# Batches of edges on every second step of the first group's chain, and turned rows of the early mixes loaded by pairs of tiles

## The reference

```
xn = layernorm(x)
msg = (xn @ weight[rel])[rel_type, src] * norm * sigmoid(gate[rel_type, src])
agg = segment_sum(msg, dst)                     # one row of 256 per edge, added by node
mix = linear attention over all nodes: k and v normalised per head, q @ (k'v / n) @ w_out + b_out
x2 = x + relu(agg) + mix
out = x2 + moe(layernorm(x2))                   # 8 experts, gelu, the best 2 of 8 by a softmax
```

## Time and profile before

| what | value |
| --- | --- |
| median of the runs, before | 1965.0 us (3 runs, 1964.9 to 1967.81) |
| profiled execution, its own time | 1951.6 us |
| its span | 1949.8 us |
| mean granted clock of TensorE | 0.968 |
| PE busy | 1797.4 us (92%) |
| DVE busy | 1201.1 us (62%) |
| ACT busy | 890.4 us (46%) |
| POOL busy | 798.1 us (41%) |

### The profile page before, as it was taken

How to read it: one execution, slowest core, us unless ns; L and a number is a source line. 1 busy time by engine, 2 the same in 40 slices (tenths; PEclk the granted TensorE clock), 3 DMA queues, 4 the chain that set the end, 5 groups by cost and what they waited for, 6 DMA issues and landing times.

```text
span 1949.8 us, 27534 instructions
## 1 busy us (share of the span) xinstructions
PE 1797.4 (92%) x9513; PEld 1525.9 (78%) x9513; DVE 1201.1 (62%) x3560; ACT 890.4 (46%) x1712; POOL 798.1 (41%) x823
## 2 busy tenths in 40 slices
PE   6999999999998699988789989999999899999898
PEld 5878888888887577776578878788888788878788
DVE  6564445444444567666566676776777767767565
ACT  5555566555553333332135444354454443534454
POOL 2000000000002366666666656666666656557600
PEclk8999999999999799999889999999999999999999
DMA  6566777655555644444653333334334333333310
GB/s 215 227 232 233 289 284 265 253 219 205 205 218 207 241 130 133 130 136 143 220 153 97 102 92 95 107 88 124 112 103 129 91 110 117 93 114 97 109 23 17
DMA packets 123550, 300.07 MB, mean 154 GB/s; under 512 B 18794, under 2 KB 82160, under 8 KB 114836
## 3 DMA queue, kind: packets, MB, share of 16 engines
q1 hardware_dynamic: 84788, 193.83, 27.2%
q0 software_dynamic: 38624, 104.48, 18.5%
HBM read 164.82 MB, written 133.42 MB: 153 GB/s over the span
## 4 chain that ended last, share of the span: by engine, by line
PE 70%; DVE 11%; another core or an unknown queue 7%; issue 5%; ACT 5%; DMA 1%; SPq 0%; DVEq 0%; ACTq 0%
PE bank L50 19%; PE bank L52 18%; PE bank L51 18%; PE bank L1480 9%; DVE rest L929 2%; ACT squares L1236 1%; DVE onehot_norm L900 1%; DVE parts L714 1%; PE bank L1475 1%; PE bank L1368 1%; PE bank L1463 1%; DVE agg L1081 1%; PE bank L1477 1%; DVE rest L1047 1%
## 5 line engine op out<-in xcount | busy, mean ns | idle before, releaser
L683 POOL DMA_INDIRECT msg<-messages,idxT x784 | 783.9, 1000 | 1044.5 <-issue 799.4
L50 PE MATMUL bank<-parts 128*128 128x512 f32 (+2 forms) x2180 | 817.3, 375 | 36.1 <-issue 12.6
L52 PE MATMUL bank<-parts 128*128 128x512 f32 (+2 forms) x2180 | 771.0, 354 | 7.0 <-issue 6.9
L51 PE MATMUL bank<-parts 128*128 128x512 f32 (+2 forms) x2180 | 770.9, 354 | 5.5 <-issue 5.1
L50 PEld LDWEIGHTS bank<-parts 128*128 128x128 f32 x2180 | 418.9, 192 | 94.5 <-issue 25.0
L52 PEld LDWEIGHTS bank<-parts 128*128 128x128 f32 x2180 | 418.0, 192 | 64.7 <-issue 10.2
L51 PEld LDWEIGHTS bank<-parts 128*128 128x128 f32 x2180 | 419.1, 192 | 60.2 <-issue 10.5
L1284 ACT ACTIVATE rest<-bank,small 128x512 f32<-128x512 f32 (+1 forms) x208 | 133.5, 662 | 385.1 <-PE bank L52 204.8
L1480 PE MATMUL bank<-msg,onehot_norm 128*128 128x256 f32 x1176 | 300.7, 392 | 6.9 <-issue 6.4
L1177 ACT ACTIVATE plain<-bank,plain 128x256 f32<-128x256 f32 x392 | 163.7, 469 | 248.3 <-PE bank L52 246.0
L757 DVE TENSOR_SCALAR plain<-bank,plain 128x256 f32<-128x256 f32 x392 | 171.0, 478 | 165.0 <-PE bank L52 111.2
(11 more groups left out here) (190 smaller groups left out, 1516.5 us busy)
## 6 DMA issues: line engine op xcount, KB each, us to landing
messages<-plain SPq DMA_DIRECT2D x49, 2048.0 KB, 7.3
parts<-xnT_scratch SPq DMA_DIRECT2D x14, 1024.0 KB
xnT_scratch<-parts SPq DMA_DIRECT2D x98, 128.0 KB, 3.3
msg<-messages,idxT POOLq DMA_INDIRECT x784
w_parts<-piece_parts SPq DMA_DIRECT2D x32, 256.0 KB, 2.4
parts<-w_parts SPq DMA_DIRECT2D x4, 2048.0 KB
mix_parts<-xnT_scratch SPq DMA_DIRECT2D x15, 512.0 KB
plain<-in_x SPq DMA_DIRECT2D x48, 128.0 KB, 7.3
```

The lines of the kernel that those rows point to most:

```text
L50: e.matmul(out, left(0), right(0), start=start, stop=False)
L51: e.matmul(out, left(0), right(1), start=False, stop=False)
L52: return e.matmul(out, left(1), right(0), start=False, stop=stop)
L683: e.indirect_dma_start(msg[:, b % SLOTS, j, :], None, table_rows, bass.IndirectOffsetOnAxis(idxT[:, j, b:b + 1], 0)).then_inc((s_gather if ...
```

## The change

Two things are changed in the program's text.

In the chain of group 0 a batch stood behind each of the 13 steps; now one stands only behind the steps with an even i, seven in all. The six others are not dropped: `share()` spreads 143 batches over its 178 places where it spread 137.

The turned rows of the early mixes are loaded by two tiles, 512 KB, for each early mix, into one of the two halves of `xnT_early`. Each half has a semaphore. The load for early mix n waits only for early mix n-2. On SP the first two stand at `fold` 0, and each other one at the step of early mix n-2, ahead of that step's store.

```
@@ order
         ready(0, i)
         if i in EARLY_AT:
             order.append(("early_mix", EARLY_AT[i]))
-        more()
+        if i % 2 == 0:
+            more()
     order += [("up", 0, 0), ("weigh", 0, 0)]
@@ semaphores
-        s_early_xnT, s_early_x = sem("early_xnT"), [sem(f"early_x{i}") for i in range(2)]
+        s_early_xnT, s_early_x = ([sem(f"early_{n}{i}") for i in range(2)] for n in ("xnT", "x"))
@@ sync_program
             def load_early_xnT(n):
-                if n:
-                    e.wait_ge(s_early_sum, 2 * n)
-                e.dma_start(raw(xnT_early), xnT_dram[EARLY[n], :, :, :, :]).then_inc(s_early_xnT, 16)
+                if n >= 2:
+                    e.wait_ge(s_early_sum, n - 1)
+                half = slice(2 * (n % 2) * P, 2 * (n % 2) * P + 2 * P)
+                e.dma_start(raw(xnT_early)[:, :, :, half], xnT_dram[EARLY[n // 2], :, :, :, half]).then_inc(
+                    s_early_xnT[n % 2], 16)
...
                     load_mix(0)
-                    load_early_xnT(0)
+                    for n in range(2):
+                        load_early_xnT(n)
...
                     if 1 <= a[0] < len(EARLY_MIXES) - 1:
                         load_early_x(a[0] + 1)
-                    if a[0] % 2 and a[0] + 1 < len(EARLY_MIXES):
-                        load_early_xnT((a[0] + 1) // 2)
+                    if a[0] + 2 < len(EARLY_MIXES):
+                        load_early_xnT(a[0] + 2)
                     store_early(a[0])
@@ tensor_program
             def early_mix(n):
-                e.wait_ge(s_early_xnT, 16 * (n // 2 + 1))
+                e.wait_ge(s_early_xnT[n % 2], 16 * (n // 2 + 1))
```

## The result

The change made the kernel slower: 1981.55 us as the median of seven runs (1975.01 to 1992.07) against 1964.19 us for seven runs of the kernel before on the same chip (1954.61 to 1967.81). The ratio is 1.0083, with a 95% interval of 1.005 to 1.0115. Its profiled execution took 1975.01 us. The ratios in this document are those on record for each comparison, and not always the quotient of the two medians.

The account below looks back on a forecast made before the run. Waits, not PE's work, were taken to bound group 0's chain, and PE the experts' part. Waits removed -22.0, new +15.2, bunches +1 gave -5.8 us, taken as -7: 1958 us, range 1946 to 1969.

Parts of the forecast that it names:

- the first of the change part by part: Six batches move from the chain to the experts' part: 8.1 us of PE's work taken out and added, sum zero.
- wrong in its balance if the experts' part grows by under 5 or over 12 us: Sign set beforehand for the experts' part, which was expected to be longer by 8 to 9 us.
- The bunches: Four and three batches together ahead of the first mix of groups 9 and 10: 1 us, bounds 0 and 4.1.
- Rival 4: Experts' part takes the six batches partly for nothing, in PE's idle time: 4 us below forecast, 1954 us; chance 0.08.
- the slower one: In the chain, PE's signals stay late and the cover is gone: +9.5 us, 1974 us; chance 0.15.
- Loads: Waits for turned rows ahead of early mixes 2, 4 and 6: 1 us left for all three, bounds 0 and 4.
- if the waits for turned rows stay: Sign that the first term, on PE's waits for turned rows in the chain, is wrong: SP's order, not size, holds them.
- Turns: New waits of PE ahead of the two `turn_norm` steps in the chain: 3.5 and 1.0 us.
- the choice: New wait of PE ahead of `turn_choice` in the chain, behind DVE's work: 1.0 us.
- rival 1: In the chain, signals are late only where a batch stands behind, and the clock holds: -17 us, 1948 us; chance 0.17.
- Rival 3: Chain and experts' part cancel, nothing that can be told: 0 +- 4 us, 1965 us; chance 0.20.
- fourth part: Waits that replace the removed ones at handoffs out of PE in the chain: 11.1 us, plus 3.1 us of clock.

Follow-up runs that it names:

- `f_rows`: Only the loads by pairs of tiles changed, against the kernel before, on a chip of about 1800 us: 1796.72 us, 0.9989.
- The even placement: Whole change with the experts' batches spread so none is forced in, against the kernel before: 1799.77 us, 0.9999; later 0.9995 and 0.9997.
- chip b: Chip of the second comparison of the whole change with the kernel before: 1961.42 us against 1936.95, 1.0152.
- `r_after`: The whole change run again beside the kernel before on another slower chip: 1961.42 us, 1.0152; its profiled execution took 1954.78 us.

## Why the prediction was wrong

The forecast was 1958 us (range 1946 to 1969), and 1981.55 us were measured. **The step that failed** is the first of the change part by part: "One costs PE 1.35 us ... taken out at one place and added at the other: the sum starts at zero". It holds on the chips of 1800 us (-6.9 and +7.2 us). Where before takes 1937 us or more, it doesn't: the experts' part grew by 34.8 and 22.3 us in the two profiles, where 8 to 9 were forecast. It is 938.0 - 850.0 = 88 us longer there with the same 137 batches, by division 0.64 us a batch on top of 1.35. That this surcharge belongs to the batches is read from where it is missing: the last group but one, with two batches, takes 48.1 us in before and 49.6 in `f_rows`, and the last group, which has none, takes 36.7 us in both (the first row from before, whose span ends at 1949.8 us, the second from `f_rows`, 1796.8 us):

```profile
1913.06 0.62 PE L1601 MATMUL bank<-parts 48*128 48x256 f32 x3
```

```profile
1760.10 0.62 PE L1604 MATMUL bank<-parts 48*128 48x256 f32 x3
```

With 143 batches the surcharge is 0.81 us each in one profile (972.9 - 857.1 = 115.8) and 0.72 in the other. So six batches go with neither 6 x 1.35 = 8.1 us nor 6 x 2.0 = 12, but with 22 and 35: by this arithmetic the others became dearer too. The prediction's own mark, "wrong in its balance if the experts' part grows by under 5 or over 12 us", was met. The cause of that growth stays open. The bunches alone aren't it, since 15.0 and 11.9 us of it stand in the seven groups that have none; the density, the places of the batches and the earlier start of the experts' part are left. The even placement was timed only where there is no surcharge, and the two profiles put the growth in different groups.

**The experts' part as something that takes on work at PE's price**: I read 799.96 of 856.10 us as "paid nearly in full". The 56 us that were left were not a reserve: the same part has 11 us on the chips of 1800 us (849.97 - 838.55), and the rest goes with the late handoffs of the others. Rival 4 had that with the wrong sign. None of the rivals let the experts' part grow by more than the work moved, and the slower one put all its loss in the chain.

**The waits removed and added**: the sum of the chain came near (-17.5 us here, -12.7 on chip b, where about -15 was forecast, six batches included), by compensation. Loads: 1 us was left, bounds 0 and 4; it was 4.7 us behind `parts<-xnT_scratch` and 3.4 more ahead of the same line. "3.1 us if time goes with bytes" failed, with 5.2 us for 512 KB; and I followed mixes 2, 4 and 6 alone, though 3 and 5 wait as well. The prediction's own mark was "if the waits for turned rows stay (then SP's order, not the size, holds them)", and the rows of SP bear it out: each half stands behind a load of x that waits for a store. The Trainium skill, page "DMA: Bandwidth & Descriptors", section "Anatomy of one DMA", would give 3.2 us for a load of 512 KB, an estimate from its fit. The rows have 5.2 at a DMA share of 0.75, and the measurement decides. Turns: 3.5 + 1.0 us were forecast, none came in the first profile. DVE's row of mix (0, 1) shows why:

```profile
953.40 0.69 DVE L977 SCALAR_TENSOR_TENSOR agg<-agg,bank 128x512 f32<-128x512 f32 x1 [1.91 <-PE bank L52]
```

It starts as PE begins what comes next (953.29 us), not 9.7 us late. That was luck of the execution: in `r_after` the same signal is late again, by about 5 us (PE turns to early mix 2 at 943.86 us), and the turn waits 2.5 us:

```profile
948.59 0.69 DVE L977 SCALAR_TENSOR_TENSOR agg<-agg,bank 128x512 f32<-128x512 f32 x1 [6.54 <-remote]
954.63 0.63 PE L1549 MATMUL bank<-ident,rest 128*128 128x128 f32 x4 [2.50 <-issue]
```

In the first profile `route` waited 0.66 us (3.0 forecast), the choice 0 (1.0), the second `up` 2.69 (2.6). That is nearer to rival 1's chain than to the forecast's, with dearer loads; `r_after` lies between the two. The short lateness of `route`, which spoke for rival 1, is no more than a bound: DVE was busy with a batch until 990.0 us, so it couldn't have taken the signal sooner than 989.96 us. The clock stayed at 0.88 instead of coming half back.

**The bunches** were put at 1 us (0 to 4.1); on the 1800 us chips their removal is worth nothing that can be told.

**Rival 3**, nothing happens, is what the chips of 1800 us show (1799.22 against 1799.41): chain and experts' part cancel there, as it said, though with no late signals at all.

## What to carry to other kernels

Work that is moved out of a stretch full of waits isn't free where it lands: for 8.1 us of work the part that took it grew by 7.2 us on the chips where it was 99% busy, and by 22 and 35 us on those where it was 93% busy. Read first whether the idle 7% is one wait or many short ones. Here it was many short ones, and they became more with the work. When batches left the chain, the next cover to fall was the one over the loads, and halving a load of 1 MB saved under 1 us of its 6; what else stands ahead of a load in its queue mattered more. A change of less than 1% wants more than one chip, and both of its halves alone: here the loads alone are the better kernel, by little (0.9971 to 0.999 on three chips, no difference to be told on a fourth), and the batches only lose where they were run alone.

## What the runs showed of the hardware

The same kernel takes 1798 to 1802 us on four of the chips met, and 1937 to 1964 us in three comparisons on two or three others. The first 600 us, in which no gather runs, are alike: PE is busy for 580.5 to 582.3 us of them in the profiles of both kinds. Behind them the profiles differ by one word, "remote", which stands for a release for which the profile finds no instruction that had just ended. Such releases in the kernel before, 1015 to 1790 us (waiting engine and line, total us, times, longest):

```profile
ACT rest L1284 <- remote: 111.8, 22, 13.3
POOL msg L683 <- remote: 47.4, 26, 2.8
DVE agg L1081 <- remote: 33.9, 17, 3.9
```

All five profiles kept on the slower chips have such rows, 144 to 156 in each, and the fifteen on 1800 us chips have none. The granted clock differs with them: 0.97 against 1.00 in the experts' part. Late signals of PE (9.7 us in the earlier trace rows, 11.6 us above), on which the prediction spent its fourth part, are thus a property of some chips; it is not settled what they are. They come only beside the gathers and batches: all of them lie between 627 and 1880 us, the gathers of the same profiles between 612 and 1877 us, and the last group takes the same 36.7 us on both kinds. The Trainium skill, page "Perfetto Trace Analysis", section "Per-engine timelines", has the semaphore move only at PSUM's acknowledgement; no run here shows why that should take 10 us on one chip and none on another.
